# A two-layer decoder on one Trainium2 core: self attention's engines reordered, operand loads spread over a stage, and latent attention's turns and values one slot later

## The reference, cut to what matters

```python
x = ln(x + L0_attn(x))                     # self attention: 4 branches x 16 heads of 16, causal
x = ln(x + L0_xattn(x, ctx, ctx))          # 16 heads over 361 context rows
x = ln(x + L0_ffn(x))                      # adapter chosen per sequence
x = ln(x + L1_attn(x))                     # hashed buckets
x = ln(x + L1_xattn(ctx, x, mask))         # latents: 16 heads of 64 over 361 + 100 keys
x = ln(x + L1_ffn(x))                      # routed experts

# L0_attn, per head:
w = softplus(q @ k.T * s / |k|);  w = where(causal, w, 0);  w = w * sigmoid(pi/sqrt(3) * w)
alpha = 1 / (sum(w) + sink + 1e-6);  out = (w * alpha) @ v + sink * alpha * v_null
# L1_xattn: kv from concat(ln(ctx), ln(x)), q from ln(x), softmax, out-projection, ln, residual, ln
```

## Time and profile before

| | |
|---|---|
| median of 3 runs | 2555.2 us (2553.42 to 2560.78) |
| the profiled execution's own time | 2563.16 us |
| its span, first to last instruction | 2561.5 us |
| mean granted TensorE clock | 0.912 of full speed |
| busy share of the span | PE 83%, DVE 53%, PE weight loads 51%, ACT 44%, POOL 19% |
| instructions | 48525 |
| self attention | 40 to 590 us |
| cross attention | 590 to 1034.5 us |
| adapter, bucket attention | 1034.5 to 1358 us |
| latent attention | 1358 to 2290 us |
| routed experts | 2290 to 2561.5 us |

### The profile page before, as it was taken

The page is one execution under the profiler, slowest core; times in us unless marked ns, Lnnn a source line. Parts: engine busy times, 40 slices in busy tenths (PEclk is TensorE's granted clock), DMA queues, the critical chain, the costliest instruction groups (busy, mean ns, idle before and its releaser), DMA issues. The chain is left out here.

```text
span 2561.5 us, 48525 instructions
## 1 busy us (share of the span) xinstructions
PE 2135.1 (83%) x17362; PEld 1314.8 (51%) x17363; DVE 1355.6 (53%) x3264; ACT 1128.6 (44%) x2404; POOL 474.4 (19%) x533
## 2 busy tenths in 40 slices
PE   1888888864999999777777999999999999963992
PEld 0454555442666665554443555655555555552661
DVE  1577777751455555358883455555555555432223
ACT  0566666650555555135552444444444444420110
POOL 2455555510000000224440000000000000003002
PEclk9789999975999999779997999999999999966996
DMA  5000000006000000000000000000000000026101
GB/s 153 1 2 1 0 0 0 2 1 185 19 18 12 17 15 2 1 1 0 0 0 18 7 7 6 6 6 12 6 6 6 6 6 7 1 78 223 33 31 58
DMA packets 50461, 60.83 MB, mean 24 GB/s; under 512 B 9849, under 2 KB 44974, under 8 KB 49918
## 3 DMA queue, kind: packets, MB, share of 16 engines
q1 hardware_dynamic: 47366, 53.74, 6.8%
q0 software_dynamic: 3008, 5.91, 0.8%
HBM read 51.11 MB, written 8.52 MB: 23 GB/s over the span
## 5 line engine op out<-in xcount | busy, mean ns | idle before, releaser
L2155 DVE CUSTOM_DVE_ANT_0 la_pr<-la_pS,la_mb 100x461 f32<-100x461 f32 x256 | 148.1, 636 | 197.2 <-PE la_pS L2018 197.2
L2000 PE MATMUL la_side<-la_wkv,la_inT 128*128 128x512 f32 (+1 forms) x512 | 243.4, 598 | 0.0
L2256 ACT ACTIVATE la_pr<-la_pr,la_nm 100x461 f32<-100x461 f32 x256 | 171.9, 674 | 135.8 <-DVE la_nm L2155 135.8
L1988 PE MATMUL la_side<-la_inT,la_wkv 128*128 128x461 f32 x512 | 227.2, 566 | 0.8 <-ACT la_inT L2240 0.8
L2264 ACT COPY la_pT<-la_pPT 128x400 f32<-128x400 f32 x256 | 126.2, 493 | 165.4 <-PE la_pPT L2026 164.1
L2026 PEld LDWEIGHTS la_pPT<-io_ident,la_pr 100*128 100x128 f32 x1024 | 110.4, 144 | 149.0 <-issue 105.7
L1028 DVE TENSOR_REDUCE ca_nm<-ca_pS 100x2 f32<-100x722 f32 x128 | 116.2, 908 | 112.5 <-PE ca_pS L915 110.6
L2323 POOL TENSOR_TENSOR la_xb<-io_X,la_bo 100x256 f32<-100x256 f32 x16 | 11.6, 728 | 840.4 <-DVE io_X L2144 840.4
L2026 PE MATMUL la_pPT<-io_ident,la_pr 100*128 100x100 f32 x1024 | 137.5, 257 | 29.7 <-ACT la_pT L2264 18.4
L1100 ACT ACTIVATE ca_pr<-ca_pS,ca_nm 100x361 f32<-100x361 f32 x256 | 130.0, 561 | 64.4 <-DVE ca_nm L1028 62.6
L2117 DVE COPY la_v<-la_side 128x512 f32<-128x512 f32 (+1 forms) x128 | 87.8, 686 | 101.3 <-PE la_side L2000 101.2
(11 more groups left out here) (356 smaller groups left out, 4372.7 us busy)
## 6 DMA issues: line engine op xcount, KB each, us to landing
rf_w<-in_L_ffn_W SPq DMA_DIRECT2D x16, 1024.0 KB, 14.0
ca_cn<-in_ctx SPq DMA_DIRECT2D x16, 256.0 KB
la_cn<-in_ctx SPq DMA_DIRECT2D x16, 256.0 KB, 2.7
rows_in<-io_zero SPq DMA_DIRECT2D x20, 128.0 KB, 4.6
rb_xr<-rows_in POOLq DMA_DIRECT2D x20, 128.0 KB, 2.3
rows_out<-rb_yr SPq DMA_DIRECT2D x20, 128.0 KB, 1.7
ea_wcT<-in_t_L_ffn_conv_W SPq DMA_DIRECT2D x1, 2048.0 KB
la_wkv<-in_L_xattn_Wkv SPq DMA_DIRECT2D x1, 2048.0 KB
```

The lines of the kernel that those rows point to most:

```text
L1988: last = nc.tensor.matmul(pf[:, 0:SK], wkv[:, k, e * P:(e + 1) * P], inT[:, k, :], start=k == 0, stop=k == KD - 1)
L2000: last = nc.tensor.matmul(pf[0:keys[c], :], inT[:, k, c * P:c * P + keys[c]], wkv[:, k, o:o + 512], start=k == 0, stop=k == KD - 1)
L2155: ins = nc.vector.tensor_tensor_reduce(out=pr[m % 2][:, e, 0:SK], in0=pS[0:T, 2 * (m % 2) + e, 0:SK], in1=mb[b][:, :], scale=-1.0, scalar= ...
L2256: ins = nc.scalar.activation(pr[m % 2][:, e, 0:SK], pr[m % 2][:, e, 0:SK], ACT.Exp, scale=-1.0, bias=nm[m % 2][:, e:e + 1], accum_out=zs[m ...
```

## The change

Self attention: `sm` has two buffers, so `masked(s, 0)` waits for the softpluses of batch s-2 only. DVE: softplus 1 and 2 of a batch move into the next body (behind `masked(s, 0)` and behind `context_read`), softplus 0 in front of `normalised(v, 3)`; `normalised(v, 2)` goes ahead of `normed`. ACT: sigmoid 5 and logarithm 0 go ahead of the fourth `values_read` and of `qT_read`. POOL: the first step of q's rope goes ahead of `k_scaled`.

```diff
-                def masked(s, c):
+                def masked(s, b, c):
                     if c == 0:
-                        above(dv, s_W, s * NPT)
+                        above(dv, s_W, (s - 1) * NPT)
...
                     if S:
-                        masked(s, 0)
+                        masked(s, par, 0)
+                    if V:
+                        softplus(v, other, 1)
                     if F:
                         k_biased(f)
                     if O:
                         context_read(o)
+                    if V:
+                        softplus(v, other, 2)
...
+                    if V:
+                        normalised(v, 2)
                     if O:
                         normed(o)
-                    if V:
-                        normalised(v, 2)
                     if F:
                         kT_read(f, other)
+                    if S:
+                        softplus(s, par, 0)
                     if V:
                         normalised(v, 3)
                     if N:
                         xT_read(f + 1, par)
-                    if S:
-                        softplus(s, par, 0)
-                        softplus(s, par, 1)
-                        softplus(s, par, 2)
...
                         sigmoid(s, par, 4)
+                    if S:
+                        sigmoid(s, par, 5)
+                        logarithm(s, par, 0)
                     if V:
                         values_read(v, 3)
-                    if S:
-                        sigmoid(s, par, 5)
                     if F:
                         qT_read(f, other)
                     if S:
-                        logarithm(s, par, 0)
                         logarithm(s, par, 1)
                         logarithm(s, par, 2)
...
                     if F:
+                        q_roped(f, 0)
                         k_scaled(f)
-                        q_roped(f, 0)
                         q_roped(f, 1)
```

```diff
-                load(0)
-                for x in later:
-                    x.load(sp)
-                for i in range(1, 3):
+                todo = [(x, t, src) for x in later for t, src in x.pairs]
+                share = -(-len(todo) // (NB - 4))
+                for i in range(NB):
                     load(i)
-                with sp.Fori(3, NB) as i:
-                    load(i)
+                    if i:
+                        for x, t, src in todo[(i - 1) * share:i * share]:
+                            x.one(sp, t, src)
...
+    w.cn = st.sb("cn", [P, 3, D])
+    w.pairs += [(w.cn[:, 0:2, :], d["ctx_1024"][0, 0:2 * P, :].rearrange("(c p) n -> p c n", p=P)),
+                (w.cn[0:SC - 2 * P, 2, :], d["ctx_1024"][0, 2 * P:SC, :])]
```

```diff
-    ORDER = [["by", "fk0", "fv00", "fk1", "fv01"], ["fk2", "fv10", "fk3", "fv11", "fq0"],
-             ["fk4", "fv20", "fk5", "fv21", "fq1"], ["fk6", "fv30", "fk7", "fv31", "gl", "gc0", "gc1"]]
+    ORDER = [["fk0", "fk1", "fk2", "fq0", "fk3"], ["by", "fv00", "fk4", "fv01", "fk5"],
+             ["fv10", "fk6", "fv11", "fk7", "fv20"], ["fq1", "fv21", "fv30", "fv31", "gl", "gc0", "gc1"]]
...
-        pr = [sb(f"pr{b}", [T, 2, KP_]) for b in range(2)]
+        pr = [sb(f"pr{b}", [T, 2, KP_]) for b in range(4)]
...
-                        if j:
-                            both_values(i, b, j - 1)
+                        if j > 1:
+                            both_values(i, b, j - 2)
                         elif not first:
-                            both_values(i - 1, 1 - b, MD - 1)
+                            both_values(i - 1, 1 - b, j + 2)
                         scores(i, b, 2 * j)
                         scores(i, b, 2 * j + 1)
...
+                        for h in range(4):
+                            some(h + 1)
+                            if j:
+                                turn(i * MP + 2 * j - 2 + h // 2, 2 * j - 2 + h // 2, h % 2)
+                            elif not first:
+                                turn(i * MP - 2 + h // 2, MP - 2 + h // 2, h % 2)
+                        some(9)
...
                         maxima(i, b, 2 * j)
                         maxima(i, b, 2 * j + 1)
+                        some(2)
                         norm(i * MP + 2 * j, 2 * j)
-                        some(2)
+                        some(4)
                         norm(i * MP + 2 * j + 1, 2 * j + 1)
-                        some(3)
-                        if j == 1 and not first:
+                        if j == 2 and not first:
                             out_norm(i - 1)
-                        if j == 2 and not first:
+                        if j == 3 and not first:
                             x_norm(i - 1)
                         if j == 2 and ahead:
                             inputs(i + 2)
                         if j == 3 and ahead:
                             apply_inputs(i + 2)
...
                         for h in range(4):
-                            if h:
-                                some(2 + h)
-                            evac(i * MP + 2 * j + h // 2, h // 2, h % 2)
+                            some(h + 1)
+                            if j:
+                                evac(i * MP + 2 * j - 2 + h // 2, h // 2, h % 2)
+                            elif not first:
+                                evac(i * MP - 2 + h // 2, h // 2, h % 2)
+                            if h < 2:
+                                exps(i, 2 * j + h)
...
-                residual(0)
-                stage(2)
-                residual(1)
-                with po.Fori(2, NB - 1) as i:
-                    stage(i + 1)
+                stage(2)
+                residual(0)
+                with po.Fori(1, NB - 2) as i:
+                    stage(i + 2)
                     residual(i)
```

More of the change, by code:

```diff
@@ L81, in want, with one @@
         return t
+    def one(self, sp, t, src):
+        with self.st.nc.allow_non_contiguous_dma("small constants"):
+            dst = t[0:src.shape[0]] if len(t.shape) == len(src.shape) else t[:].rearrange("p a b -> p (a b)")
+            sp.dma_start(dst, src).then_inc(self.s_in, 16)
     def load(self, sp):
[L84 to L87, removed]
+        for t, src in self.pairs:
+            self.one(sp, t, src)
     def wait(self, eng):
@@ L227, in self_attention @@
         kTm = [sb(f"kTm{b}", [P, KD, 2, P]) for b in range(2)]
-        sm = sb("sm", [P, NS])
+        sm = [sb(f"sm{b}", [P, NS]) for b in range(2)]
         L = [sb(f"L{b}", [P, NS]) for b in range(2)]
@@ L571, in body @@
                     if S:
-                        masked(s, 2)
+                        masked(s, par, 2)
                     if F:
@@ L575, in body @@
                     if S:
-                        masked(s, 3)
+                        masked(s, par, 3)
                     if V:
@@ L1849, in __init__ @@
         self.g, self.f = [n for n in self.names if n[0] == "g"], [n for n in self.names if n[0] == "f"]
-        assert self.per % 2 == 0 and kinds[0] == "b" and kinds.count("b") == 1
+        assert self.per % 2 == 0 and kinds.count("b") == 1
         self.lead = 2 * len(self.g) + len(self.f) - 1
@@ L1860, in at @@
         if isinstance(i, int):
-            gone = len(self.g) if i == NB - 1 else 0
-            return self.At(self.lead + self.per * i + k - gone, None, self.per)
+            back = next(q for q, n in enumerate(self.names) if n[0] == "b")
+            if i == 0:
+                k += k < back
+            elif i == NB - 1:
+                k -= len(self.g) + back
+            return self.At(self.lead + self.per * i + k, None, self.per)
         return self.At(self.lead + k, i, self.per)
@@ L1958, in load @@
                     sp.dma_start(cn[0:ckeys[2], 2, :], d["ctx_1024"][i, 2 * P:SC, :]).then_inc(s_cn, 16)
-                for i in range(3):
+                for i in range(1, 3):
                     load(i)
@@ L2011, in scores @@
                     if m == 0:
-                        turns.wait_read(pe, s_R, i, "fk7")
+                        turns.wait_read(pe, s_R, i, "fv30")
                         turns.wait_read(pe, s_R, i, "fv31")
@@ L2054, in body, with some @@
                         todo = turns.steps(i, j)
-                        for h, upto in enumerate((2, 3, 4, 5)):
+                        def some(upto):
                             while todo and todo[0][0] < upto:
@@ L2058, in body @@
                                 step(name, n, i + turns.AHEAD[name[0]], turns.buffer(name, b))
-                            turn(i * MP + 2 * j + h // 2, h // 2, h % 2)
-                        for _, name, n in todo:
-                            step(name, n, i + turns.AHEAD[name[0]], turns.buffer(name, b))
+                        for h in range(4):
[5 more added lines that the diff above has]
+                        some(9)
                 w.wait(pe)
@@ L2066, in _ @@
                 over_batches(pe, body, 3)
+                both_values(NB - 1, 1, MD - 2)
```

(7 more changed lines are left out.)

43 lines of the change are left out of this document (21 added, 22 removed).

## The result

| | before | after |
|---|---|---|
| median of 11 runs, us | 2554.4 (2550.7 to 2560.8) | 2563.4 (2558.4 to 2566.4) |
| profiled execution (span), us | 2563.2 (2561.5) | 2565.4 (2563.6) |
| self attention ends (last row of X written) | 588.5 | 557.9 |
| cross attention ends | 1034.5 | 979.6 |
| adapter and bucket attention end | 1357.6 | 1297.6 |

The changed kernel is slower: ratio 1.0031, 95% interval 1.0019 to 1.0042, 9.0 us by the medians. Forecast were 2543.0 us and "faster"; the time lies in the range of 2510 to 2578, the direction was wrong. Self attention wins 30.6 us and cross attention 24.3 (446.0 to 421.7), the adapter and bucket stages in between 5.1 (323.1 to 318.0); latent attention loses 60.1 (930.6 to 990.7) and what follows 2.0. The sum for this pair of executions is +2.1; the profiled execution of before happened to be 9 us over the median of the table, that of after 2.

A forecast was written before the change was run, and what follows sets the result against it. PE set the order in self attention, with waits, and bounded latent attention; cross attention waited 24.00 us for a load. Terms -42 - 31 + 61 = -12 gave 2551 from the profiled 2563.2, 2543 from the median; range 2510 to 2578.

The forecast's parts named there:

- Latent, +61: Latent attention: 78 us added by gl's wait in 14 bodies, less 12.3, 2.4 and 2 won; 39 to 90.
- the clock's price: Latent slot 3: low clock after gl's 3.46 us wait costs 1.55 us a body (0 to 3.3).
- The first rival: Latent slot 3: gl's wait costs more, 7.3 us a batch, 102 in all, total 2568, slower; chance 0.24.
- Self attention, -42: Self attention: 33 us from 13 cycles of 28.2 instead of 30.73, 2 at the start, 7 at the end.
- I take 0.4 of a fall at 2.2, 0.9: Self cycle: 0.4 clock falls at 2.2 us each add 0.9 to 27.3, giving 28.2.
- The start: Self attention's first two cycles: POOL comes up to 1.9 us earlier, 2 us gained (0 to 4).
- the tail: Self attention's last two cycles: output projection waits less, about 3.5 us each, 7 gained (4 to 9).
- The rival with a fall in each cycle: Self attention: every cycle keeps a clock fall, 28.85 us, 33 won instead of 42, total 2552, no change; chance 0.20.
- Cross attention, -31: Cross attention: earlier second context load wins 24.0 us of wait and 6.9 of low clock, 30.9 together (26 to 32).
- the 6.9 of low clock: Cross attention, behind the second tile: 15.15 us busy at clock 0.51 become 7.7 at full clock, less 0.5 of waits.
- no operand share delays a later load: Cross attention: 31 operand loads, three to a batch behind load(i), a share taking 13 us of 23, cost nothing.
- The rule weighed in the prediction: Self attention: by the skill's rule each new cycle would hold a clock fall, winning some 9 us less.

The follow-up runs named there:

- the doses: Changed kernel with fv31 read only after apply_inputs (1.53 us wait left): 2526.2 us; with inputs applied straight behind slot 3's first norm (no wait): 2492.4 us.

## Why the prediction was wrong

By its own steps:

- **Latent, +61: right.** Profiles +60.1, alone +65.6. The period came out as forecast (60.0), gl's wait as 3.59 for 3.46, the clock's price as 1.92 for 1.55, and PE waits for gc1 0.31 us on the mean for the 0.56. VectorE's apply took 1.46 for three operations, where I had counted 1.05. That VectorE's order is the cause is shown by the doses: with 3.59, 1.53 and 0 us of wait a batch took 60.0, 57.6 or 56.1, and 54.57. The first rival (7.3 a batch or more) had the place right and the price too high; that its total of 2568 lies nearer to 2563.4 than mine is luck, for the missing microseconds are those of the next two points.
- **Self attention, -42: the failed step.** At full clock a cycle takes 26.91, forecast 27.3; but "I take 0.4 of a fall at 2.2, 0.9" was wrong in both factors. Seven of thirteen cycles have a fall (0.54), and it costs 3.9 on the mean (about 4.25 in six of them, 1.65 in the first), 2.09 a cycle. So thirteen cycles from 115.01 to 492.04 took 29.00 each instead of 28.2: 22.5 won instead of 33. That the waits of 0.85 and 1.36 us at the cycle's end bring the falls is shown by the runs that fill them: none of thirteen cycles has one with both filled, three with one multiplication in each. The low stretches of before do last about as long as I read from the mean clock (3.4 and 6.8 us); the error was to carry their price over. My own rows had the dear fall (3.3) in the cycles where the small waits brought it, and the cheap one (1.55) behind the long wait; I wrote that the new waits are like the former and then took a value between the two. And even 3.3 was too low, since the new low stretch lasts 10.2 us where the longest of before lasted 6.8. The start came out 3.8 early against 2 forecast, the tail 4.2 against 7. Together -30.6 in this pair of profiles, -28.6 alone. The rival with a fall in each cycle (28.85) was nearest in the period by luck: the falls were fewer, and each far dearer.
- **Cross attention, -31: one term wrong.** The wait of 24.0 is gone. Of the 6.9 of low clock behind it almost nothing is won in the changed kernel: PE worked at half clock for 15.7 us behind the wait before (636.9 to 652.6) and does so for 13.2 now (584.5 to 597.7), with waits on ACT and DVE of 0.5 to 0.65 between its steps from 574 to 586. With cross attention's edits alone it is about 7 us. I had taken the 24 us wait for the only cause of the low clock, and it was not. That no operand share delays a later load is borne out by the profile: of PE's two DMA waits in the stage, 26.0 us together before, only the 1.9 for the very first tile is left.
- **The rule weighed in the prediction.** By the rule of the Trainium skill (TensorE: Matmul & The Clock Gate, "HAM oscillation") a wait that recurs in every tile throttles in every tile. The page tells it of a DMA wait that is longer than the tile's work. In latent attention the trace agrees: behind waits of 3.59 us the clock falls in each of the 14 bodies, for 3.4 or 6.8 us. In self attention, with its shorter waits, it falls in seven cycles of thirteen. The 9 us that the rule would have cost this part are near the 11 to 13 that were missed, but they were missed mostly by longer falls, and by a few more of them.
- **The base.** The sum went from the profiled execution of before, 8 us over the median. Misses by term, in the profiles and then in the kernels with one part each: self 11 and 13 us, cross 7 and 1, latent -1 and 5; in the profiles the stages that were not changed give back 3. That turns -12 into +2 (profiles) to +7 (parts), and +9.0 was measured. A forecast between two sums of 73 and 61 us had no room for misses of 10%.

Open: why the self cycle falls in every other round only while the waits are in each, why a fall lasts 3.4 us in one place and 6.8 or 10.2 in another, why cross attention keeps half clock for so long, and the 5 us of the adapter and bucket stages, whose code is the same (318.0 to 323.3 among these runs).

## What to carry to other kernels

Where one engine is busy nearly all the time, look for the shortest list of instructions that another engine has to do before it can release it, and put just that list first: here VectorE's normalisation of the later inputs, moved ahead of two reads, a norm and x_norm, was worth 71 us. When PE has short recurring waits, price the clock apart from the wait, and don't carry the price of one fall over to another place: here it was 1.55 to 3.3 us before and mostly 4.25 after. A run that fills the wait with useless multiplications separates the two, and may be worth keeping. A big gain in one stage and a big loss in another, set against each other, give no sure sign: test the stages apart.

## What the runs showed of the hardware

- Two gaps of 0.85 and 1.36 us, 2 us apart, brought PE from 2.4 to 1.2 GHz for about 10 us, at a cost of 4.25 us, in six of thirteen cycles; the same gaps one cycle later did not.
- Low stretches of about 3.4, 6.8 and 10.2 us all occur in these traces: in the changed kernel, waits of 0.85 and 1.36 us were mostly followed by 10.2, and the wait of 3.59 us by 3.4 or 6.8.
- At full clock the filled gaps held: thirteen cycles in a row to within 0.01 us (27.70).
- A 128x512 fp32 multiplication leaves two records of 0.443 us each.
- POOL's residual addition (100x256) takes 737 ns in self and 728 in latent attention before, and 931 and 984 in the changed kernel, where it runs beside other work of VectorE. With the inputs applied first, and so with another neighbour, the latent one is back at 731, the one in self attention stays at 932. Lines of the costliest groups, of the changed kernel and then of the one with the inputs applied first:
```profile
L757 POOL TENSOR_TENSOR sa_xb<-io_X,sa_bo 100x256 f32<-100x256 f32 x16 | 14.9, 931 | 0.0
L2347 POOL TENSOR_TENSOR la_xb<-io_X,la_bo 100x256 f32<-100x256 f32 x16 | 15.7, 984 | 830.9 <-DVE io_X L2164 830.9
```
```profile
L2347 POOL TENSOR_TENSOR la_xb<-io_X,la_bo 100x256 f32<-100x256 f32 x16 | 11.7, 731 | 790.6 <-DVE io_X L2164 790.6
```
The slow-down is mutual: VectorE's apply, which overlaps the addition in the changed kernel, takes 1.46 us there for three operations and 1.05 where it doesn't (rows of 1750.19 and 1715.77 above). The addition beside it:
```profile
1750.46 1.04 POOL L2347 TENSOR_TENSOR la_xb<-io_X,la_bo 100x256 f32<-100x256 f32 x1 [55.74 <-DVE io_X L2164]
```
What the two engines share was not tried by itself.
